# Head one-hots stored in DRAM during the second sort and loaded by both hyperbolic passes, with the mix split between GpSimd and VectorE in another way

## The reference

```
hyper_head = expmap0(head_emb)                  # head_emb = e[src], tail_emb = e[dst]
hyper_tail = expmap(tail_emb, hyper_head)
hyper_rel  = expmap(rel_emb, hyper_head)        # rel_emb = relation_emb[type - 1]
res = project(mobius_add(hyper_tail, hyper_rel))
res = relu(logmap(res, hyper_head) + l2_normalize(tail_emb + rel_emb) * 1e-7)
sums = zeros.at[head].add(res)                  # summed per head node, divided by the count
```

## Time and profile before

| | us |
|---|---|
| median of 3 runs | 24344.68 |
| lowest, highest | 24342.23, 24354.15 |
| profiled execution | 24370.34 |
| its span, first to last instruction | 24368.5 |

### The profile page before, as it was taken

The page is one execution under the profiler, slowest core; times in us unless marked ns, Lnnn a source line. Parts: engine busy times, 40 slices in busy tenths (PEclk is TensorE's granted clock), DMA queues, the critical chain, the costliest instruction groups (busy, mean ns, idle before and its releaser), DMA issues. The chain is left out here.

```text
span 24368.5 us, 206631 instructions
## 1 busy us (share of the span) xinstructions
PE 12002.2 (49%) x52285; PEld 10009.4 (41%) x52286; DVE 9424.1 (39%) x14053; ACT 2083.8 (9%) x3841; POOL 16775.5 (69%) x16828
## 2 busy tenths in 40 slices
PE   3233434677757777576764435344334434334333
PEld 1111222566646666466663335333333323333333
DVE  6555444688868888511111112111111121111112
ACT  0000001233322322100010001000000000000000
POOL 4777777788847777577727772777477757774775
PEclk6555566555555555555555555555555555555555
DMA  0000001222222222211111111111211121121112
GB/s 23 2 2 10 26 25 50 51 59 57 57 42 56 56 55 56 38 27 27 27 14 28 28 28 13 28 28 28 21 28 28 28 27 28 28 26 23 28 28 27
DMA packets 756517, 765.78 MB, mean 31 GB/s; under 512 B 442786, under 2 KB 522854, under 8 KB 736348
## 3 DMA queue, kind: packets, MB, share of 16 engines
q0 software_dynamic: 528384, 511.86, 13.4%
q1 hardware_dynamic: 227932, 251.96, 3.3%
HBM read 659.46 MB, written 103.37 MB: 31 GB/s over the span
## 5 line engine op out<-in xcount | busy, mean ns | idle before, releaser
L447 POOL DMA_INDIRECT rows<-table_lin,pay x9984 | 9444.2, 946 | 4814.9 <-issue 3026.1
L1427 DVE TENSOR_TENSOR acc<-acc,pair 128x1024 f32 x832 | 1016.1, 1221 | 10646.5 <-PE pair L671 10604.7
L671 PE MATMUL pair<-rows,onehot 128*128 128x64 f32 x19968 | 4798.9, 425 | 0.0
L671 PEld LDWEIGHTS pair<-rows,onehot 128*128 128x128 f32 x19968 | 4492.3, 332 | 520.3 <-issue 520.3
L659 PE MATMUL pair<-ones_bf,zeros_bf 1*128 1x512 bf16 x1664 | 837.6, 604 | 7794.9 <-issue 7789.6
L447 POOL DMA_INDIRECT rows<-table_hyp,pay x3328 | 3324.8, 999 | 1240.9 <-issue 993.8
L659 PEld LDWEIGHTS pair<-ones_bf,zeros_bf 1*128 1x128 bf16 x1664 | 109.8, 100 | 7923.2 <-issue 7923.2
L431 POOL DMA_INDIRECT payload_src<-rows x1600 | 1559.2, 974 | 738.8 <-issue 738.8
L634 PE MATMUL pair<-tab,sel_t 128*128 x6656 | 1560.0, 409 | 979.1 <-ACT head L832 404.9
L431 POOL DMA_INDIRECT payload_dst<-rows x1600 | 1563.5, 977 | 499.0 <-issue 487.5
L634 PEld LDWEIGHTS pair<-tab,sel_t 128*128 128x128 f32 x6656 | 1366.0, 304 | 1263.3 <-issue 1263.3
(11 more groups left out here) (301 smaller groups left out, 15183.3 us busy)
## 6 DMA issues: line engine op xcount, KB each, us to landing
rows<-table_lin,pay POOLq DMA_INDIRECT x9984, 2.4
rel<-rel_rows SPq DMA_DIRECT2D x52, 1072.0 KB
xs<-rel_rows SPq DMA_DIRECT2D x52, 1072.0 KB
rows<-table_hyp,pay POOLq DMA_INDIRECT x3328
rel_rows<-rel SPq DMA_DIRECT2D x26, 1072.0 KB
rel_rows<-xs SPq DMA_DIRECT2D x26, 1072.0 KB
payload_src<-rows POOLq DMA_INDIRECT x1600, 2.1
payload_dst<-rows POOLq DMA_INDIRECT x1600
```

Source lines behind the costliest of these rows:

```text
L447: pool.indirect_dma_start(out=rows[:, h, t, 0:width], out_offset=None, in_=table[:, :], in_offset=bass.IndirectOffsetOnAxis(ap=pay[:, h, t ...
L671: last = nc.tensor.matmul(sums[:, bass.ds(at, D)], onehot[:, h, t, :], mv, start=False, stop=False, skip_group_check=True)
L1427: V.tensor_tensor(flat_acc[:, at], flat_acc[:, at], ps_half[u], ALU.add)
```

## The change

- In the second sort, `types` on DVE makes two more operations for each group: the one-hot of the head's place for each half, into two staging halves (`hot_half`: the tile `msg` and a free stretch of `onehot`), each after a wait for the store that last read the staging half. `types_made` now counts three for each group.
- SP stores each half (1024 KB) to `head_hots` in DRAM (`store_hot`), ahead of the relation rows of the pair; 104 stores.
- In both hyperbolic passes DVE no longer makes `onehot` (the type one-hot stays in its place). SP loads each half from `head_hots` after the relation rows, as soon as PE has used up that half (`scattered`); 208 loads. PE's `turn` waits for that load (`hot_moved`) in place of `hot_made`.
- POOL's `mix` only multiplies, in two halves of 16 tiles. DVE makes both additions: behind head + tail it waits for POOL's multiplication of this half (`mixed`) and adds the relation rows, for half 0 and then for half 1, and signals `coefficients` only then. ACT's relu waits for `coefficients`, and so does SP's load of the next relation rows.

```diff
@@ SP
+            def store_hot(i, h, u):
+                await_reg(sp, "sp", types_made, 6 * i + (3 * h + u + 2))
+                sp.dma_start(head_hots[bass.ds(4 * i + (2 * h + u), 1)].rearrange("a q c -> (a q) c"), hot_half[u]).then_inc(hot_moved[h][u], 16)
+            def load_hot(m, i, h, u, free):
+                if free:
+                    await_reg(sp, "sp", scattered, 4 * i + (m * SUMMED + 2 * h + u - 3))
+                sp.dma_start(onehot[:, h, half(u), :].rearrange("p t n -> p (t n)"),
+                             head_hots[bass.ds(4 * i + (2 * h + u), 1)].rearrange("a q c -> (a q) c")).then_inc(hot_moved[h][u], 16)
             def types_pair(i, free):
                 for h in range(2):
                     if free:
-                        await_reg(sp, "sp", types_made, 2 * i + (h - 1))
+                        await_reg(sp, "sp", types_made, 6 * i + 3 * (h - 1))
                     load_pay(0, i, h)
+                for h in range(2):
+                    for u in range(2):
+                        store_hot(i, h, u)
                 for h in range(2):
                     store_rel(i, h)
...
-                            await_reg(sp, "sp", S["mixed", m], MIXES * 2 * i + MIXES * (h - 1))
+                            await_reg(sp, "sp", S["coefficients", m], MIXES * 2 * i + MIXES * (h - 1))
                             load_rel(i, h)
+                            for u in range(2):
+                                load_hot(m, i, h, u, True)
@@ POOL, mix
-                hd, rl = head[h][:, :, 0:D], rel[h][:, :, 0:D]
-                await_reg(pool, "pool", S["coefficients", m], MIXES * g + 1)
-                nc.gpsimd.tensor_tensor(rl, rl, over(EO[:, 3, :], D), ALU.mult).then_inc(S["mixed", m], 1)
-                await_reg(pool, "pool", S["mixed", m], MIXES * g + 1)
                 for u in range(2):
-                    await_reg(pool, "pool", S["coefficients", m], MIXES * g + (u + 2))
-                    nc.gpsimd.tensor_tensor(hd[:, half(u), :], hd[:, half(u), :], rl[:, half(u), :], ALU.add).then_inc(S["mixed", m], 1)
+                    rl = rel[h][:, half(u), 0:D]
+                    if u == 0:
+                        await_reg(pool, "pool", S["coefficients", m], MIXES * g + 1)
+                    nc.gpsimd.tensor_tensor(rl, rl, over(EO[:, 3, half(u)], D), ALU.mult).then_inc(S["mixed", m], 1)
@@ PE, turn
-                    await_reg(pe, "pe", hot_made, 2 * g + (m * HOT + q // (QG // 2) + 1))
+                    await_reg(pe, "pe", hot_moved[h][q // (QG // 2)], 16 * i + ((m + 1) * LOADED + 16))
@@ ACT, relu
-                        await_reg(act, "act", S["mixed", m], MIXES * g + (u + 2))
+                        await_reg(act, "act", S["coefficients", m], MIXES * g + (u + 2))
@@ DVE, types in the second sort
                 dve.drain().then_inc(types_made, 1)
+                for u in range(2):
+                    for k in range(2):
+                        if k < h or turned:
+                            await_reg(dve, "dve", hot_moved[k][u], 16 * i + (16 if k < h else 0))
+                    V.tensor_tensor(hot_half[u].rearrange("p (t n) -> p t n", n=P), over(pay[:, h, half(u), 1], P),
+                                    ps_sort_iota.unsqueeze(1).to_broadcast([P, HG, P]), ALU.is_equal)
+                    dve.drain().then_inc(types_made, 1)
@@ DVE, end of messages
                     level()
-                    TT(th, th, tr, ADD)
+                    ttl(th, th, tr, ADD)
+                    await_reg(dve, "dve", S["mixed", m], 2 * g + (u + 1))
+                    TT(th, th, rl[:, half(u), 0:D], ADD)
                     dve.drain().then_inc(S["coefficients", m], 1)
                 dve.sem_inc(rows_free, 1)
@@ DVE, make_half_hot
-                V.tensor_tensor(onehot[:, h, t, :], over(pay[:, h, t, 1], P),
-                                ps_iota.unsqueeze(1).to_broadcast([P, HG, P]), ALU.is_equal)
```

More of the change, by code:

```diff
@@ L169, in build @@
         st_u = st_us[0]
+        hot_half = [flat_msg[:, 0:HG * P], flat_hot[:, 5900:5900 + HG * P]]
         HB = NB // 2
@@ L210, in build @@
         rel_moved = [sem(f"rel_moved_{h}") for h in range(2)]
+        hot_moved = [[sem(f"hot_moved_{h}_{u}") for u in range(2)] for h in range(2)]
+        transposed, sel_copied = sem("transposed"), sem("sel_copied")
+        TURNS = GROUPS * QG
         types_made, types_turned, types_kept, rel_made, rel_kept = (
@@ L217, in build @@
             if n < 2:
-                for m in ("transposed", "sel_copied", "fetched", "fetch_copied", "asked", "answered", "coefficients", "mixed"):
+                for m in ("fetched", "fetch_copied", "asked", "answered", "coefficients", "mixed"):
                     S[m, n] = sem(f"{m}_{n}")
@@ L362, in _ @@
                 sp.wait_ge(rel_moved[h], LOADED)
+                for u in range(2):
+                    sp.wait_ge(hot_moved[h][u], LOADED)
             meet(sp, BN["prep0"])
@@ L616, in _, with turn @@
             sum_regs = [pe.alloc_register(f"sum_block_{j}") for j in range(HG)]
[L618 removed]
+            def turn(m, i, h, q):
+                g = 2 * i + h
                 if q % (QG // 2) == 0:
[L621 removed]
+                    await_reg(pe, "pe", hot_moved[h][q // (QG // 2)], 16 * i + ((m + 1) * LOADED + 16))
                 if q > 1:
[L623 removed]
+                    await_reg(pe, "pe", sel_copied, g * QG + (m * TURNS + q - 1))
                 for j in range(4):
                     last = nc.tensor.transpose(ps_sel[q % 2][:, j * P:j * P + P], onehot[:, h, 4 * q + j, :], ident[:, :])
[L626 removed]
+                last.then_inc(transposed, 1)
             def fetch(m, g, h, q):
                 await_reg(pe, "pe", S["fetch_copied", m], g * QG + (q + 2))
[L631 removed]
+                await_reg(pe, "pe", sel_copied, g * QG + (m * TURNS + q + 1))
                 for j in range(4):
@@ L636, in fetch, with fetch_group @@
                 last.then_inc(S["fetched", m], 1)
-            def fetch_group(m, g, h):
-                turn(m, g, h, 0)
-                turn(m, g, h, 1)
+            def fetch_group(m, i, h):
+                g = 2 * i + h
+                turn(m, i, h, 0)
+                turn(m, i, h, 1)
                 for q in range(QG):
```

20 lines of the change are left out of this document (9 added, 11 removed).

## The result

The kernel took 24345.01 us before and takes 24778.06 us now (medians of four runs each, 24342.23 to 24354.15 and 24769.67 to 24780.88; the ratio is 1.0177, with an interval of 1.0159 to 1.0194). The forecast was 24747, in a range of 24550 to 24880. The profiled execution of the changed kernel has a span of 24776.0 us.

What follows compares the result with a forecast made beforehand. A loop of gather, multiplication, DVE's additions, `rows_free` and `pay` was to take 55.05 us a group against 50.34 and 51.94; 391 + 6 + 5 = 402 us more gave 24772 profiled, 24747 as median, range 24550 to 24880.

Steps and rivals of the forecast that it cites:

- Gather: POOL's gather in the hyperbolic passes: 41.0 to 42.0 us a group, taken as 41.5, collisions with DVE's line 1272 staying.
- The rival with an undisturbed gather: POOL's gather not slowed by DVE: 39.5 us, loop 53.05 us, time 24547 us; chance 0.08.
- Two halves of the multiplication: POOL's split multiplication in each group: 3.65 to 4.34 us for the pair, taken as 4.0.
- DVE's addition of half 0: DVE's first relation-row addition finds POOL at its second half and ends 1.1 us after that half.
- slipped in between the halves: Rival: DVE's addition starts before POOL's second half, loop 53.33 us, time 24575 us; chance 0.20.
- the step to the multiplication: On POOL, from the gather's end to the multiplication: 0.05 us a group.
- DVE's half 1: DVE's remaining work on the second half, all behind the addition of half 0: 5.25 us a group.
- From `rows_free` to the gather: From DVE's signal through SP's load of `pay` to POOL's next gather: taken as 3.15 us a group.
- Loads of the one-hots, "nothing": Two 1024 KB loads a group in the hyperbolic passes, about 5.5 us each, costed at nothing on the path.
- The total: Whole kernel: 391 us for the passes, 6 for their last groups, 5 for the sort; 402 us more.
- The second sort: 104 one-hots and stores covered by DVE's idle time; 5 us added for the start, bounds 0 and 45.
- The faster case: `rows_free` and `pay` come before POOL's multiplication ends: 45.7 us a group, time 23812 us; chance 0.05.

Runs made afterwards that it cites:

- the moved kernel: The changed kernel with 45 empty DVE drains ahead of pass 0 and 40 ahead of pass 1; 24749.70 us, ratio 1.0165.
- early indices: The changed kernel with SP loading `pay` for group g+2 once group g's coefficients are there, without waiting for `rows_free`; 24569.08 us, ratio 1.0074.
- the fastest kernel: The changed kernel with `rows_free` signalled before DVE waits for POOL's product, plus 45 and 40 empty DVE drains ahead of passes 0 and 1; 24220.18 us, ratio 0.9949.
- the moved kernel before: The kernel before the change with 40 empty DVE drains ahead of its pass 1 and nothing else; 24254.20 us, ratio 0.9962.

## Why the prediction was right

The mechanism was the forecast's. Between the profiled executions the loss is 407.4 us; 402 had been summed. Of the 31 us between 24747 and the measured 24778, 25.66 are the step by which the profiled execution of the kernel before was set off against its median; the changed kernel's profiled execution lies on its median.

- *Gather.* 41.5 taken; busy and idle time give (1678.5 + 484.2) / 52 = 41.6 in pass 0 and 41.7 in pass 1. The rival with an undisturbed gather had 39.5 and fell. In the two passes of the changed kernel 196 DMAs of the gathers take more than 1.4 us, and each of them lies beside a large DVE operation with two operands in SBUF; of the 2739 with none beside them the longest takes 1.05. One that meets DVE's line 1305 takes 2.35 us in place of 0.95:

```profile
5574.75 2.28 DVE L1305 TENSOR_TENSOR msg<-xs,rows 128x2048 f32<-128x2048 f32 x1
5575.50 2.35 POOL L474 DMA_INDIRECT rows<-table_hyp,pay  x1 [0.30 <-issue]
```

- *Two halves of the multiplication.* 4.0 taken from between 3.65 and 4.34; 3.77 measured, near the low end. Half a multiplication costs about half of it (1.92), and not what the addition of its size costs (2.17).
- *DVE's addition of half 0*, 1.1 behind POOL's end: 5621.05 - 5619.96 = 1.09. DVE never slipped in between the halves, so that rival fell too: its addition starts 2.06 us after the start of POOL's first half, which lasts 1.92, so POOL is already at its second. With the step to the multiplication the three terms come to 4.88 where 5.15 had been summed.
- *DVE's half 1.* 5.25 taken, 5626.31 - 5621.05 = 5.26.
- *From `rows_free` to the gather.* 3.15 taken, 3.06 at one half of the groups and 3.7 to 3.8 at the other (medians). This is the term that was sized too small: at the jump of DVE's loop the load of `pay` takes 0.6 to 0.7 us longer, and the moved kernel has 3.1 to 3.2 at all groups.
- *Loads of the one-hots, "nothing".* True of PE's wait, which is what the forecast had looked at (0 us in the loop). But the passes take about 0.4 us a group more with the full loads, 40 us, in gather DMAs that meet DVE's sum; the forecast had no term for that.
- *The total.* It is better than the terms, and that is luck. The two passes cost 253.4 + 176.5 = 430 us where 391 + 6 had been summed, 33 more. The stage of the sorts came out 7.7 lower where 5 had been added, and the rest, which the change doesn't touch, 14.8 lower; no run shows why. That leaves 5 of the 33.
- *The second sort.* Bounds 0 and 45, 5 taken. The step with two groups of the earlier trace rows now has 8.6 or 9.1 us of idle time left of 20.04, as the sum of 9.6 and some more for stores had it. That the stage came out 7.7 earlier is no gain of the change: the first sort, which it doesn't touch, already ended some 5 us earlier.
- *The faster case.* It was to decide at 9.6 us between the end of one gather and the start of the next. The changed kernel has 13.2 and 14.0, early indices 11.1 (slower than before), the fastest kernel 7.9 (faster than before), so the point was right. Its price was not: 45.7 us a group was POOL's sum, and the case never summed DVE, which needs 49 to 50 with the two collisions. So 24220 came out of it, with the code moved too, and not 23812.
- *Pass 1 of the kernel before*, 51.94 against 50.34. The forecast took it as it stood, and rows 7 show POOL early and waiting for `pay`. It did not ask why pass 1 differs from pass 0. The answer is the jump of DVE's loop. The sum held all the same, because it was built from the terms of the new loop, which the jump enters only through the load of `pay`.

## What to carry over

When work moves from one engine to another, write down the loop from the start of one big step to its next start, with every signal and small DMA in it: here POOL lost 5.3 us of work a group and the loop grew by 5, because the release of a buffer had come to stand behind a wait for POOL itself. Moving that release ahead of the wait was worth some 510 us, and only then did the saving on the other engine count. Before an edit is credited with a gain, look at the packets of the instruction queue in both traces: code that merely lies elsewhere moved this kernel by 90 us.

## What the runs showed of the chip

- A DVE loop of 330 to 350 instructions was fetched anew in each round, about five packets of 8192 bytes, when it touched four blocks of 128 instructions, and not when it touched three; 28 loops of fourteen kernels have no exception. Each such jump took 3.7 to 4.3 us instead of 1.2 (187.6 / 24 = 7.8 in one kernel). The Trainium skill (Runtime: NRT & Kernel Launch, "Instruction fetch mechanics") says that an engine's instruction memory holds two blocks of 256 instructions, and that a taken branch to a target outside it has to fetch. The refetch agrees. The block doesn't: the packets have 8192 bytes, and with borders every 256 instructions no place of them parts the 28 loops into those that are refetched and those that aren't, while borders every 128 do. Two of the kernels have their loops of pass 1 begin only five instructions apart, at 1853 and at 1858, one with 107 packets and the other with 6.
- A refetch on DVE also delayed a transfer that SP had issued: the gather behind `pay` started 3.3 to 3.4 us after the issue by the medians, instead of 2.7. How the two are linked isn't shown.
- A DVE addition of two SBUF operands that meets POOL's multiplication stands still and POOL doesn't: 2.80, 4.4 and up to 5.3 us instead of 1.23, while the 104 multiplications of half a group with h = 0 in the two passes lie between 1.904 and 1.927 us. It holds even where DVE had begun 0.58 us earlier. POOL doesn't always go unharmed: in pass 1 of the moved kernel before, the whole multiplication took 3.93 us in the middle instead of 3.65. The Trainium skill (SBUF — State Buffer, "Who interferes with whom") has the contention; on its inference that descriptor generation is left alone the measurement decides otherwise, 2.35 against 0.95 us, and 196 of 196 long DMAs beside such an operation.
- One of the chips ran both kernels in some 32.5 ms, with PE idle at "issue" for 533 us ahead of a line that elsewhere has 0. The cause isn't shown.
